# A retention of f32 column tiles: who evicts the score banks, who multiplies the mask, and a new order of the work

## The reference

```
x = x + retention(layernorm(x), ctx, ctx)        # 16 heads of 16
x = x + ffn_fp8(layernorm(x), kernel, ...)       # one 256x256 product in e4m3 values
x = x + cross_attention(layernorm(x), ctx, ...)  # 16 heads of 16, softmax over 512
x = x + mixture_of_experts(layernorm(x), ...)    # 8 experts, 4 chosen, gated, 512 wide

# retention: q and k are rotated and scaled by position (xpos), then
scores = einsum('bhsd,bhtd->bhst', q, k) * D     # D[n, m] = gamma_h ** (n - m) where n >= m, else 0
out    = einsum('bhst,bhtd->bhsd', scores, v)    # v = ctx, not rotated, no softmax
```

## Time and profile before

| | |
|---|---|
| median of 3 runs | 1160.15 us (1153.69 to 1160.89) |
| profiled execution, its own time | 1159.08 us |
| its span | 1157.2 us |
| mean granted TensorE clock | 0.852 |
| TensorE, VectorE, ScalarE, GpSimd busy | 948.6, 762.3, 441.2, 300.2 us |

### The profile page before, as it was taken

The page is one execution under the profiler, slowest core; times in us unless marked ns, Lnnn a source line. Parts: engine busy times, 40 slices in busy tenths (PEclk is TensorE's granted clock), DMA queues, the critical chain, the costliest instruction groups (busy, mean ns, idle before and its releaser), DMA issues. The chain is left out here.

```text
span 1157.2 us, 16807 instructions
## 1 busy us (share of the span) xinstructions
PE 948.6 (82%) x6088; PEld 514.7 (44%) x6088; DVE 762.3 (66%) x1251; ACT 441.2 (38%) x746; POOL 300.2 (26%) x309
## 2 busy tenths in 40 slices
PE   1653457878787888787754999999999999999997
PEld 1442133325432442232142565656656566565654
DVE  5454658775978687656215577777777677776765
ACT  2231134455455635445512133433333343333332
POOL 5460333035200520000000023332322323232232
PEclk9855656877879877896766599999999999999999
DMA  6413321132022303201006001010101010000001
GB/s 220 127 34 110 95 84 56 47 94 81 20 92 74 93 2 129 61 15 56 2 18 222 1 1 56 1 56 1 56 1 55 1 55 0 26 29 1 1 20 55
DMA packets 58152, 62.01 MB, mean 54 GB/s; under 512 B 9240, under 2 KB 52128, under 8 KB 58080
## 3 DMA queue, kind: packets, MB, share of 16 engines
q1 hardware_dynamic: 58080, 61.07, 16.7%
HBM read 44.13 MB, written 16.91 MB: 53 GB/s over the span
## 5 line engine op out<-in xcount | busy, mean ns | idle before, releaser
L1340 PE MATMUL gu_ps<-xt,w 128*128 128x512 f16 x1536 | 356.6, 382 | 9.5 <-DVE w L1222 9.5
L1195 POOL TENSOR_TENSOR h<-prod,h 128x512 f16<-128x512 f32 x128 | 148.3, 1159 | 400.6 <-ACT h L1168 400.6
L1340 PEld LDWEIGHTS gu_ps<-xt,w 128*128 128x128 f16 x1536 | 151.1, 99 | 167.9 <-DMA xt<-xt_d 9.8
L772 DVE TENSOR_REDUCE neg_max<-sc 128x2 f32<-128x1024 f32 x128 | 156.4, 1222 | 52.0 <-PE sc L964 50.3
L1354 PE MATMUL dn_ps<-w,h 128*128 128x256 f16 x1536 | 188.5, 273 | 1.5 <-POOL h L1195 1.5
L579 ACT ACTIVATE p<-st 128x512 f32<-128x512 f32 x256 | 138.6, 594 | 121.6 <-PE st L985 121.4
L1354 PEld LDWEIGHTS dn_ps<-w,h 128*128 128x128 f16 x1536 | 150.1, 98 | 46.1 <-POOL h L1195 2.1
L1164 ACT ACTIVATE glu<-gate 128x512 f32<-128x512 f32 x128 | 80.7, 631 | 205.4 <-DVE gate L1243 203.1
L1168 ACT ACTIVATE h<-prod 128x512 f16<-128x512 f32 x128 | 80.6, 630 | 135.1 <-DVE prod L1252 133.3
L1252 DVE SCALAR_TENSOR_TENSOR prod<-up,glu 128x512 f32<-128x512 f32 x128 | 108.8, 850 | 12.3 <-DVE up L1246 1.4
L964 PE MATMUL sc<-kz,sq 48*128 48x512 f16 x256 | 64.8, 471 | 50.1 <-DVE neg_max L772 38.8
(11 more groups left out here) (146 smaller groups left out, 868.3 us busy)
## 6 DMA issues: line engine op xcount, KB each, us to landing
raw<-in_gate_up_t SPq DMA_DIRECT2D x8, 1024.0 KB, 5.0
stack_d<-t SPq DMA_DIRECT2D x32, 128.0 KB, 1.8
raw<-in_down_t SPq DMA_DIRECT2D x8, 512.0 KB, 6.0
sq<-stack_d SPq DMA_DIRECT2D x48, 64.0 KB, 2.2
kz<-stack_d SPq DMA_DIRECT2D x48, 64.0 KB, 2.2
sq<-stack_d SPq DMA_DIRECT2D x96, 32.0 KB, 1.8
kz<-stack_d SPq DMA_DIRECT2D x96, 32.0 KB, 1.8
ctx_n<-in_ctx SPq DMA_DIRECT2D x4, 512.0 KB, 4.1
```

Source lines behind the costliest of these rows:

```text
L772: dve.tensor_reduce(neg_max[:, qt, :, pair], sc[:], AX.X, ALU.max, negate=True).then_inc(m_max, 1)
L1195: pool.tensor_tensor(h16[1][:, u % 4, :], prod[:, u % 2, :], h16[0][:, u % 4, :], ALU.subtract).then_inc(h_lo, 1)
L1340: ins = pe.matmul(gu_ps[:, 2 * (u % 2) + g, :], w[k][wi][:, col:col + P], xt[xi][:, c, kd, :], start=(j == 0 and kd == 0), stop=(j == 2 an ...
```

## The change

Scores stay in f32 from the bank on. ScalarE copies each score bank into `rm` (`r_evict`), GpSimd multiplies `causal` into it in place (`r_mask`), and `r_outs` multiplies with f32 operands: the stationary tile is 32 columns of the unsplit context (the head's 16 and the next 16, which end in unused rows), the moving one the masked scores, so that four heads lie side by side in 32-column tiles of the array and the output comes out turned. One call of `r_outs` takes two chunks. `r_take` (ScalarE) copies its bank, `r_back` (TensorE) turns it back with four transposes, and `r_add` (VectorE) adds the 128x256 that belong to x. `split_ctx`, `split_ctx_low`, `r_high`, `r_low`, `v0` and `rs` are gone, RM is 6. The state tiles are spread to 32 columns a head with zeros between. Beside that: `x_p` exists twice (x of batch b+2 is loaded in its place), the normalisations have tiles and semaphores of their own, q's normalised x lies in `x_r`, the quantiser works in `x_n` and `x3`, `values` writes 17 rows of a tile instead of 32, `next_ctx` waits for `r_outs`, and `ORDER` is written anew.

```diff
-RM = 4
+RM = 6
...
             def next_ctx(b, _):
-                sp.wait_ge(v0_lo, b + 1)
+                sp.wait_ge(r_out, (b + 1) * 4)
...
             def next_x(b, _):
...
-                if b < LAST:
-                    sp.wait_ge(ln_out, (b + 1) * 3)
+                if b + 2 < B:
+                    sp.wait_ge(ln_out[2], b + 1)
                     sp.wait_ge(x_mid, (b + 1) * 16)
-                    load_x(b + 1)
+                    load_x(b + 2)
...
# gpsimd
-            def r_low(b, arg):
+            def r_mask_(b, arg):
                 half, c = arg
...
                 for g in range(2):
-                    n = half * 8 + c * 2 + g
-                    pool.wait_ge(r_hi, b * 16 + n + 1)
-                    pool.tensor_tensor(rs[1][:, c % 2, 4 * g:4 * g + 4, :], rm[:, n % RM],
-                                       rs[0][:, c % 2, 4 * g:4 * g + 4, :], ALU.subtract).then_inc(r_lo, 1)
+                    m = b * 16 + half * 8 + c * 2 + g
+                    pool.wait_ge(r_evict, m + 1)
+                    pool.tensor_tensor(rm[:, m % RM], rm[:, m % RM], causal[:, None, :].to_broadcast([P, 4, P]),
+                                       ALU.mult).then_inc(r_mask, 1)
# scalar
-            def r_high(b, arg):
+            def r_evict_(b, arg):
                 half, c = arg
                 for g in range(2):
...
+                    m = b * 16 + half * 8 + c * 2 + g
+                    act.wait_ge(r_sc, m + 1)
+                    need(act, r_out, (m - RM) // 4 + 1)
+                    act.activation(rm[:, m % RM].rearrange("p h n -> p (h n)"), bank("r_scores", arg, g),
+                                   ACT.Copy).then_inc(r_evict, 1)
+
+            def r_take_(b, arg):
+                half, cc = arg
+                n = b * 4 + half * 2 + cc
+                act.wait_ge(r_out, n + 1)
+                need(act, r_back, n - 1)
+                act.activation(o_r[:, n % 2, :], bank("r_outs", arg), ACT.Copy).then_inc(r_take, 1)
# vector
-            def r_mask_(b, arg):
...
             def r_add_(b, arg):
-                half, c = arg
-                dve.wait_ge(r_out, b * 8 + half * 4 + c + 1)
-                xs = x_p[:, c, half * P:(half + 1) * P]
-                dve.tensor_tensor(xs, bank("r_outs", arg)[:, 0:P], xs, ALU.add).then_inc(r_add, 1)
+                half, cc = arg
+                dve.wait_ge(r_back, b * 4 + half * 2 + cc + 1)
+                xs = x_p[b % 2][:, 2 * cc:2 * cc + 2, half * P:(half + 1) * P].rearrange("p t (h d) -> p t h d", d=HD)
+                back = bank("r_back", arg).rearrange("p (t h d) -> p t h d", t=2, d=2 * HD)[:, :, :, 0:HD]
+                dve.tensor_tensor(xs, back, xs, ALU.add).then_inc(r_add, 1)
# tensor
             def r_outs(b, arg):
...
+                half, cc = arg
+                to = take("r_outs", arg, (r_take, b * 4 + half * 2 + cc + 1))
+                pe.wait_ge(state_lo, b * 2 + half + 1)
+                pe.wait_ge(r_mask, b * 16 + half * 8 + cc * 4 + 4)
+                for c in range(2 * cc, 2 * cc + 2):
+                    tok = slice(c * P, (c + 1) * P)
+                    for g in range(2):
+                        cols = slice((c % 2 * 2 + g) * P, (c % 2 * 2 + g + 1) * P)
+                        if c:
+                            for j, (qi, si) in enumerate(THREE):
+                                pe.matmul(to[:, cols], state_s[si][:, half, c - 1, 4 * g:4 * g + 4, :], t0[0][qi][:, half, tok],
+                                          start=(j == 0), stop=False, skip_group_check=True)
+                        for j in range(4):
+                            pair, par = 2 * g + j // 2, j % 2
+                            col = c * D + half * P + (4 * g + j) * HD
+                            ins = pe.matmul(to[32 * j:32 * j + 32, cols], ctx_pad[:, col:col + 2 * HD],
+                                            rm[:, (b * 16 + half * 8 + c * 2 + par) % RM, pair, :],
+                                            start=(c == 0), stop=True, skip_group_check=True)
                 ins.then_inc(r_out, 1)
+
+            def r_back_(b, arg):
+                half, cc = arg
+                n = b * 4 + half * 2 + cc
+                to = take("r_back", arg, (r_add, n + 1))
+                pe.wait_ge(r_take, n + 1)
+                for i in range(4):
+                    ins = pe.transpose(to[:, i * P:(i + 1) * P], o_r[:, n % 2, i * P:(i + 1) * P], ident[:])
+                ins.then_inc(r_back, 1)
...
             def values(b, n):
...
-                    rows = slice(i * 32, (i + 1) * 32)
+                    rows = slice(i * 32, i * 32 + HD + 1)
...
 ORDER = {
-     "rotate_k": ((5,), (35,), (175,), (438,)),
+     "rotate_k": ((3,), (92,), (254,), (518,)),
...
-     "turn0": ((8, 12, 23, 30), (103, 107, 162, 171), (274, 286, 418, 432), (567, 583, 746, 760)),
+     "turn0": ((5, 10, 13, 21), (94, 99, 134, 140), (267, 271, 370, 384), (539, 590, 665, 676)),
...
-     "stack0": ((40, 64), (184, 212), (442, 495), (769, 825)),
+     "stack0": ((36, 56), (155, 184), (393, 440), (688, 748)),
...
-     "quantise": ((119, 120, 121), (313, 317, 324), (592, 595, 617), (906, 907, 927)),
+     "quantise": ((91, 93, 98), (262, 283, 287), (551, 558, 566), (864, 875, 876)),
...
-     "qk": ((32, 37, 140, 141), (145, 167, 384, 387), (396, 425, 703, 716), (741, 753, 1015, 1024)),
+     "qk": ((30, 33, 131, 136), (145, 149, 366, 380), (392, 403, 667, 685), (703, 723, 977, 987)),
...
-     "v": ((22, 26), (53, 59), (520, 529), (842, 850)),
+     "v": ((24, 28), (47, 55), (512, 520), (835, 845)),
...
-     "stack1": ((154, 157, 158, 159), (400, 404, 453, 514), (724, 727, 780, 836), (1034, 1035, 1071, 1117)),
-     "next_ctx": ((18,), (116,), (290,), (1315,)),
+     "stack1": ((152, 153, 158, 159), (386, 389, 420, 507), (696, 699, 747, 825), (996, 998, 1031, 1079)),
+     "next_ctx": ((85,), (234,), (499,), (1275,)),
```

More of the change, by code:

```diff
@@ L153, in phase_a @@
         t1 = [sb(f"t1_{i}", [P, 2, S], F16) for i in range(2)]
-        v1 = [sb(f"v1_{i}", [P, T, H, 2 * HD]) for i in range(2)]
+        v1 = [sb(f"v1_{i}", [P, T, H, HD + 1]) for i in range(2)]
         sq1 = sb("sq1", [P, 2, HP, S], F16)
@@ L199, in phase_a @@
         state_hi, state_lo = sem("state_hi"), sem("state_lo")
-        r_sc, r_mask, r_hi, r_lo = (sem(f"r_{n}") for n in ("sc", "mask", "hi", "lo"))
-        r_out, r_add = sem("r_out"), sem("r_add")
+        r_sc, r_evict, r_mask = sem("r_sc"), sem("r_evict"), sem("r_mask")
+        r_out, r_take, r_back, r_add = (sem(f"r_{n}") for n in ("out", "take", "back", "add"))
         quant = sem("quant")
@@ L237, in phase_a @@
         ARGS |= {name: TURN0 for name in ("turn0", "turn0_high", "turn0_low", "turn0_store")}
-        ARGS |= {name: chunks for name in ("r_scores", "r_mask", "r_high", "r_low", "r_outs", "r_add")}
+        ARGS |= {name: chunks for name in ("r_scores", "r_evict", "r_mask")}
+        ARGS |= {name: [(half, cc) for half in halves for cc in halves] for name in ("r_outs", "r_take", "r_back", "r_add")}
         ARGS |= {name: halves for name in ("state", "state_sum", "state_low", "turn_q", "copy_q", "linear",
@@ L875, in r_scores @@
                 n = b * 16 + half * 8 + c * 2
-                to = [take("r_scores", arg, (r_mask, n + par + 1), par) for par in range(2)]
+                to = [take("r_scores", arg, (r_evict, n + par + 1), par) for par in range(2)]
                 for pair in range(HP):
@@ L896, in r_outs @@
-                if c == 0 and half == 0:
-                    pe.wait_ge(v0_lo, b + 1)
-                for h in [2 * pair + par for par in range(2) for pair in range(HP)]:
-                    if h < 2:
-                        pe.wait_ge(r_lo, b * 16 + half * 8 + c * 2 + h % 2 + 1)
-                    col = half * P + h * HD
-                    for si, vi in THREE:
-                        ins = pe.matmul(to[:, h * HD:(h + 1) * HD], rs[si][:, c % 2, h % 2 * HP + h // 2, :],
-                                        v0[:, c, vi, col:col + HD], start=first, stop=True, skip_group_check=True)
-                        first = False
@@ L1040 @@
 N_CONST = 7
-CONSTS = 4
+CONSTS = 5
 W8_STEPS = 8
```

315 lines of the change are left out of this document (143 added, 172 removed), and 64 rows, old and new, of the table ORDER.

## The result

| | before | changed |
|---|---|---|
| median, on the same chip | 1156.92 us (1149.83 to 1160.89, 4 runs) | 1200.81 us (1194.64 to 1205.86, 4 runs) |
| ratio to before, 95% interval | 1 | 1.0384 (1.0303 to 1.0465) |
| profiled execution, span, clock | 1159.08, 1157.2, 0.852 | 1204.16, 1202.3, 0.848 |
| start of the experts' first products | 615.4 | 661.2 |

The account below looks back on a forecast made before the run. It took TensorE and VectorE, coupled by waits, to bound phase A, with VectorE having slack in retention windows. From 1159.08 us, TensorE plus 8, VectorE minus 11 and prologue 0 gave 1156 us, range 1131 to 1182.

Parts of the forecast that it names:

- VectorE's relief: Batches 1 to 3: masks and adds leaving VectorE save 32.7 us, of which 11 show as shorter time.
- TensorE's pieces: r_outs and r_back, batches 1 to 3: 15.6 us more TensorE work, half falling into idle time, so plus 8.
- the changes of shape: Between state products and column tiles, 26 a batch: taken as 0, bounds 0 to 4.2 us a batch.
- the prologue: Start of the kernel: x_p near 74, first maxima at 122 to 130 against 124.9; counted as 0.
- first scores 42.5: Prologue: first scores start near 42.5 us instead of 50.44, paced by TensorE.
- GpSimd mask 1.2 to 1.5: Retention: one 128x512 mask on GpSimd takes 1.2 to 1.5 us; 1.3 was taken.
- ScalarE about the same: High halves and a context copy go, evictions come: ScalarE's busy time stays about the same, counted as 0.
- VectorE 33 to 44 us less: VectorE's busy time falls by 33 to 44 us, as masks and adds leave it.
- Retention windows within 3 us: The retention windows of batches 1 to 3 stay within 3 us of their length before the change.
- Rival 2: TensorE paces the retention windows, its added work showing whole: plus 25, 1184 us; over 95% busy decides it; chance 0.20.
- Rival 1: VectorE paces phase A, so all 32.7 us of its relief comes back: about 1131 us; chance 0.30.
- Rival 3: GpSimd's masks stretch from 1.3 to 2.3 us and GpSimd ends each retention window: 1179 us; chance 0.08.

Follow-up runs that it names:

- best version: Changed kernel with three SyncE steps moved, two context buffers and early key rotation, state products grouped, mask on VectorE: 1.0083 of the kernel before.
- early r_back: r_take, r_back, r_add of batches 1 to 3's last chunk pair moved up: 1.0423 of the kernel before on the changed kernel, 1.0159 on the best version.

## Why the prediction was wrong, point by point

The sum gave VectorE's relief minus 11 us, and it came to nothing; and it gave too little to TensorE's pieces (plus 8), the changes of shape (0), the prologue (0) and the order of the queues (no term). Mending the last three, and taking back the move of the mask, returns 3.0 of the 3.8 points.

- **Held:** first scores 42.5 (42.0); the GpSimd mask 1.2 to 1.5 (1.27); ScalarE about the same (441.2 and 442.2); VectorE 33 to 44 us less (38.6); the experts' phase unchanged, and batch 3's attention alone too (from the 97th reduction to the experts 141.0 us, 140.1 before).
- **VectorE, minus 11: failed.** The relief bought nothing. With the mask back, and 40 us more on VectorE, the time did not rise in either order. I had turned the waits of the earlier trace rows into a gain; the score banks' wait for a mask became one for the eviction (8.5 us over 8 before, 11.1 over 12 after).
- **TensorE's pieces, plus 15.6: under-sized, and its half wrongly covered.** I had r_outs and r_back at 8.9 us a batch fast and 15.5 slow. The two kinds of call take 1.83 and 2.52 fast, 3.05 and 4.08 slow, and an r_back 0.59 and 1.05: 11.1 and 18.5 a batch. With the prediction's clock shares that would be 23.7, not 15.6 (an estimate). Without shape changes my pieces were right: grouped, a state product takes 0.064 us (0.06 foreseen) and a group's column tiles 0.255 (0.27). That half of the work is hidden and half shows was no rule either: ahead of r_outs 42.0 us showed as 0.4%, not clear of zero, and 17.8 us behind each batch's last call showed as 21.5 us.
- **The shape changes, 0: failed.** Each costs 0.12 us at the high clock and 0.14 at the low one; the 26 a batch that I counted are 3.1 and 3.6 us. Here the Trainium skill's rule on draining at a mode switch (TensorEngine Tiling (Array Packing), Key Properties) was the better guide, and the trace agrees with it in that each change costs time. In the old order grouping gained 1.0%, 12 us, at the upper end of what I had bounded; in the new one 0.4 to 0.6%, within the noise.
- **The prologue, 0: failed by 10.8 us**, outside my 122 to 130. The scores came as foreseen, but x_p at 79.7, not 74. Most of that is in the masks, which end at 73.1, not 68.6: the first of half 1 starts at 61.1, not 58.2, and the last two wait 2.1 us for scores that stand behind the first call of r_outs. The last call's 4.1 us, not 3.0, are the rest. The context's load was issued at 77.4, where I had it landed at 77.5, and the rotation stood behind `root`: the keys were rotated at 94.9, not 86 to 88. By then the quantiser ran beside it, and from x_p to x_q it took 19.8 us, against 11.9 before and 12.1 with the rotation moved up, which gave 1.0%.
- **Order outside the prologue: no term at all.** I read the new places of `qk_store` and `stack1` and counted no queue. Three moved steps were worth 0.9%. "Retention windows within 3 us" failed with it: the scores of batches 1, 2 and 3 take 31.9, 27.8 and 44.6 us, against 25.1, 27.4 and 24.4.
- **The rivals.** Rival 2 (slower, 1184) had the sign, and shape changes and prologue among its terms, but short of the measured 1201, and its mechanism is not what happened: TensorE never was 95% busy in those windows, and 42 us of TensorE time added ahead of r_outs cost 0.4%. Rival 1 is excluded by the mask experiments. Rival 3's stretch did come, but between rotation and quantiser, not in the masks; it took in the quantiser's steps with a single tensor as input as well (1.09 for 0.69).

**What stays open.** The last 0.8% of the best version. The early r_back on top of it cost 0.8% more; the stretch and the lower clock are known, their cause is not. The old order with the new form loses 4.4% without any one wait to show for it; grouping explains 1.0 of it. What the second x_p and the 17 rows of `values` do by themselves was not tried.

## What to carry to other kernels

Price TensorE work by its place in the queue, not by its sum: put into a wait it cost nothing clear of noise here, behind the last factor of a stage it cost its full length. When a change moves an engine's work, list for each moved step what stands before it on its queue and what buffer that step frees; here three steps of one DMA queue cost 0.9%, and one step of GpSimd's, with the buffer that it needed, 1.0%. Sort products by tile shape before you judge a packed form.

## What the runs showed of the hardware

- Extra f32 transposes in the waits raised TensorE's granted clock in the same stage from 0.51 to 0.78 and from 0.80 to 1.00, so that 42.0 us of added work made TensorE 18.8 us busier in the first 616 us (425.0 to 443.8). In that profile the experts start 9 us later than in the one of the kernel before; by then it is 444.4. None of the twelve executions had a mean clock under 0.870, none of the 29 of the kernel before beside them one above 0.866.
- A change between 128x128 f16 products and 32-column f32 tiles costs 0.12 us at 2.4 GHz and 0.14 at 1.2 (2.52 to 1.79 and 4.08 to 3.24 us for six fewer). From f32 to f16 at one shape it is 0.06, from f16 to f32 0.01.
- 128x256 products on GpSimd (0.73) and 128x1024 f32 sums on VectorE (1.23) that run at once, all from SBUF, take up to 1.70 and 1.63 us; 128x1024 f32 steps with one tensor as input went from 0.69 to 1.09 in the same stretch.
- The mean duration of a product is its latency here, not its share of the engine: f32 transposes with a mean of 0.30 to 0.33 us follow one another every 0.12 to 0.15 us at the high clock (nine in 1.04, the four of r_back in 0.59).
